# Attention on one Trainium2 core: the two middle batches written out straight in place of a loop

## The chip, the cores and the metric

The kernel runs on one core of one Trainium2 chip. The metric is the device time of one execution in microseconds (us), as the median of a few runs. Lower is better.

## The reference

The reference is one decoder layer over x, of 4 batches with 1024 tokens of 256 channels. Cut to what matters:

```python
x = x + attention(layernorm(x))            # 16 heads of 16, rotary, softmax over 1024 keys
x = x + cross_attention(ctx, layernorm(x)) # 77 context tokens, one head of 256
x = x + experts(layernorm(x))              # 8 experts, 512 tokens each, gelu MLP 256-1024-256
```

The change touches the attention alone, which for each batch b and head h computes

```python
s = q[b, h] @ k[b, h].T * 16 ** -0.5       # 1024 x 1024
out[b, h] = softmax(s) @ v[b, h]
```

## The kernel before, in words

The program has four stages on the chip: `project_qkv`, `attend`, `cross_attend` and `experts`. `attend` holds the softmax attention, and it is the stage that the change touches.

`attend` works through the 4 batches. In each it goes through 4 groups of 4 heads, and for each group through two halves of 512 queries. One group and one half is called a stretch here (`hg` in the code): a batch has 8 of them, and the stage has 32. In a stretch there are 8 key tiles of 128 keys (`kt`). For each key tile TensorE computes the scores of two pairs of heads (L931), ScalarE takes exp of each pair in one instruction of 128x1024 (L750, 16 in a stretch), and TensorE multiplies the result with v (L902). VectorE takes no part in this. It prepares the row maxima that are subtracted in the scores of later stretches: TensorE computes scores of the other orientation into a ring of three PSUM banks (L880, 32 in a stretch) and VectorE reduces each to a maximum (L812). These maxima run 48 items ahead of the scores. Once in a stretch VectorE combines them (L818), TensorE transposes them (L886), VectorE splits them into two parts (L825, L827), and SyncE copies them by 8 small DMAs into two rows of the q stack of the next stretch (L679). The scores of the next stretch wait for these rows (semaphore `s_row`).

GpSimd has two tasks in `attend`. In every even stretch (in the last batch only in the first) it issues 9 DMAs that load a head group's q, k and v for later (L483 and L486), and after them it multiplies the output of the stretch before last with the reciprocal sums (L551, `tail.scale`). The reciprocal sums themselves travel by DMA: L529 for the sums, L535 on VectorE for the reciprocal, L540 and L543 on SyncE to spread them, L558 on SyncE to store the result. ScalarE copies the output bank once in a stretch (L737).

The whole order is written out by hand. Each of the five engines has a function `body(i, first, last)` that emits its program of one batch, with the batch number either a Python number or a loop register. The helper `bodies` calls it. With a Python number every semaphore wait is against a constant and every DMA address is fixed. With a register these are worked out by register instructions beside the work.

At the begin of a body TensorE has the ring in the state that the body before left. `free` decides what it waits for before it writes a bank. From the fourth item on it waits for the reduction of the item three back. For the first three items of a body (`m < NR`) it waits for this:

```python
elif "items" in n:
    pe.wait_ge(s_mr, n["max"])
    pe.wait_ge(s_ra, n["rows"])
```

Here `n["max"]` is the number of all maxima of the bodies before, so the wait is for the last reduction and not for the one three back. This text is the same for a body in the loop and for one outside.

Of the kernel before, what the change touches and what calls it, by code (L numbers as in the profile page):

```python
# [14 lines left out]
B, L, C = 4, 1024, 256  # L15
# [564 lines left out]
def attend(nc, ps, ident, group0, s_clear0, stores, ends, tail, firsts, cw, s_cw, x, ost, wts, qst, kst, vst):  # L580
# [5 lines left out]
    with ctx:  # L586
# [38 lines left out]
        LATE = AHEAD // PER - KT  # L625

        def bodies(eng, body):
            body(0, True, False)
            with eng.Fori(1, B - 1) as i:
                body(i, False, False)  # L630
            body(B - 1, False, True)

        def plan(last):

# [50 lines left out]
        def _(sp):  # L685
# [16 lines left out]
            def body(i, first, last):  # L702
                n = before(i, first)
                for hg in range(NH):
# [14 lines left out]
                    if first and hg == 2:  # L719
                        load_context_weights(sp, cw, s_cw, wts)  # L720
            bodies(sp, body)
            for h in range(2):
                sp.wait_ge(tail.s_os[h], 16 * G * NG)
# [6 lines left out]
        @block.scalar  # L730
        def _(act):
            def take(m, x):

                act.wait_ge(s_pv, KT * (m + 1))
                if not (isinstance(m, int) and m < 2):
                    act.wait_ge(s_att, m - 1)
                nc.scalar.activation(osb[:, x, :], ps[:, PV, :], ACT.Copy).then_inc(s_oe, 1)  # L737

            def body(i, first, last):
                for hg in range(NH):  # L740
                    for kt in range(KT):
                        S = KT * hg + kt
                        for u in range(2):
                            if u == 1 and kt == 1 and not (first and hg == 0):
                                take(8 * i + hg - 1, (hg - 1) % 2)
                            act.wait_ge(s_st[u], 64 * i + S + 1)

                            if not first or S >= NP:
                                act.wait_ge(s_pv, 64 * i + S - NP + 1)
                            nc.scalar.activation(pr[:, S % NP, u], ps[:, 2 * u:2 * u + 2, :], ACT.Exp,  # L750
                                                 scale=D ** -0.5).then_inc(s_ex[u], 1)
            end_leading(act)
            act.wait_ge(s_ra, 1)
            rows(act, 0, 0, (1,))
            bodies(act, body)
            take(NH * B - 1, 1)

        @block.gpsimd
        def _(pool):
# [21 lines left out]
            def body(i, first, last):  # L781
                for hg in range(NH):
# [16 lines left out]
                    if hg > 1 or not first:  # L799
                        tail.scale(pool, g_, 8 * i + hg - 2, hg % 2, 4 * i + (hg - 2) // 2 + 1)  # L800
            bodies(pool, body)
            tail.scale(pool, g_, NH * B - 2, 0, NG * B)

# [1301 lines left out]
```

## Time and profile before

| | us |
|---|---|
| median of 3 runs | 1193.57 |
| the three runs | 1193.57, 1189.91, 1193.67 |
| span of the profiled execution, first to last instruction | 1188.0 |
| median less span | 5.6 |
| first exp of `attend` to the first exp of its last batch | 135.2 to 637.0 |
| TensorE busy, share of the span | 91% |
| VectorE busy, share of the span | 86% |

The span leaves out what lies before the first and after the last instruction of the program. A total for the profiled execution is not given beside its span, so the median stands for it. `attend` takes from about 120 us to about 796 us of the span. The engines' programs are joined by semaphores only, so the stage's pace is seen from the start times of one kind of instruction, here the first exp of a stretch.

### The profile page before, as it was taken

How to read it: one execution, taken by the hardware profiler on the slowest of the kernel's cores; microseconds unless marked ns; L12 is line 12 of the kernel's file. 1: busy time of each engine (PE TensorE's matmuls, PEld its weight loads, DVE VectorE, ACT ScalarE, POOL GpSimd, SP SyncE). 2: the span in 40 equal slices, each digit the busy share in tenths (PEclk: the TensorE clock that was granted, in tenths of full speed). 3: DMA queues.
4: the chain of work that ended last, by engine and by line, in shares of the span. 5: the costliest groups of instructions: out<-in, count | busy, mean ns of one | idle time of the engine just before them, and what ended most of it. 6: DMA issues, size and time to landing. Idle time of an engine off the chain costs nothing. (4 is left out here: it accounts for less than half of the span.)

```text
span 1188.0 us, 24515 instructions
## 1 busy us (share of the span) xinstructions
PE 1086.0 (91%) x8540; PEld 596.5 (50%) x8540; DVE 1021.9 (86%) x2168; ACT 767.9 (65%) x932; POOL 352.7 (30%) x316
## 2 busy tenths in 40 slices
PE   7889989999999998999999999999994059999998
PEld 6776333333333333333333333337784038888897
DVE  8999889999999998999999999827998975766663
ACT  4552368888888886788887888874555014655653
POOL 2657812202220220222022000022100022876575
PEclk9987699999999999999999999999998559999999
DMA  6786664504422440442344000036432022555433
GB/s 238 250 266 219 150 106 97 95 19 78 75 58 38 84 75 19 78 74 45 51 80 78 17 16 16 17 102 211 157 128 95 0 71 57 150 144 132 111 111 36
DMA packets 84695, 114.10 MB, mean 96 GB/s; under 512 B 25056, under 2 KB 57568, under 8 KB 84576
## 3 DMA queue, kind: packets, MB, share of 16 engines
q1 hardware_dynamic: 66256, 69.82, 19.8%
q0 software_dynamic: 15024, 36.17, 17.2%
q10 hardware_dynamic: 3296, 6.56, 1.6%
q8 instruction: 70, 1.15, 0.4%
q14 instruction: 49, 0.40, 0.1%
HBM read 73.31 MB, written 38.27 MB: 94 GB/s over the span
## 5 line engine op out<-in xcount | busy, mean ns | idle before, releaser
L812 DVE TENSOR_REDUCE b_max_halves<-banks 128x1 f32<-128x512 f32 x1024 | 627.1, 680 | 19.9 <-PE banks L880 19.7
L750 ACT ACTIVATE b_probs<-banks 128x1024 f32<-128x1024 f32 x512 | 520.4, 1026 | 153.9 <-PE banks L931 153.8
L880 PE MATMUL banks<-b_k,b_q 62*128 62x512 f32 x1024 | 399.8, 471 | 5.8 <-DVE b_max_halves L812 1.7
L931 PE MATMUL banks<-b_q,b_k 64*128 64x512 f32 x1024 | 386.9, 457 | 8.4 <-DMA b_q<-b_max_rows 5.2
L902 PE MATMUL banks<-b_probs,b_v 128*17 128x256 f32 (+1 forms) x3840 | 316.3, 402 | 0.2 <-ACT b_probs L750 0.2
L931 PEld LDWEIGHTS banks<-b_q,b_k 64*128 64x128 f32 x1024 | 157.1, 186 | 229.7 <-issue 173.3
L880 PEld LDWEIGHTS banks<-b_k,b_q 62*128 62x128 f32 x1024 | 162.2, 190 | 40.4 <-DVE b_max_halves L812 37.4
L902 PEld LDWEIGHTS banks<-b_probs,b_v 128*17 128x17 f32 x3840 | 64.0, 95 | 166.1 <-issue 99.0
L551 POOL TENSOR_TENSOR b_att<-b_out,b_rec_spread 128x512 f32<-128x512 f32 x32 | 41.0, 1283 | 307.6 <-DMA b_rec_spread<-reciprocals 307.4
L483 POOL DMA_DIRECT2D b_q<-q_stacks x60 | 31.8, 532 | 234.6 <-PE banks L902 220.9
L1851 DVE TENSOR_TENSOR e_hTl<-e_hT,e_hTh 128x512 fp32r<-128x512 f32 x64 | 47.6, 745 | 48.2 <-ACT e_hT L1605 46.6
L1631 POOL DMA_INDIRECT e_x<-rows,d_idx x32 | 45.3, 1415 | 110.1 <-DVE d_wx L1806 56.7
L1602 ACT ACTIVATE e_hTh<-banks,e_b 128x512 fp32r<-128x512 f32 x64 | 44.1, 689 | 52.0 <-PE banks L1963 48.4
L1963 PE MATMUL banks<-e_w2h,e_hTh 128*128 128x256 f32 x256 | 73.1, 286 | 0.0
L1963 PE MATMUL banks<-e_w2l,e_hTh 128*128 128x256 f32 x256 | 72.4, 283 | 0.0
L1963 PE MATMUL banks<-e_w2h,e_hTl 128*128 128x256 f32 x256 | 72.4, 283 | 0.0
L1588 ACT ACTIVATE e_xTh<-banks 128x512 fp32r<-128x512 f32 x16 | 8.7, 596 | 83.0 <-PE banks L1951 83.0
L1654 POOL DMA_INDIRECT out_x<-c_x,d_idx x32 | 55.3, 1728 | 17.7 <-DVE c_x L1884 11.0
L1963 PE MATMUL banks<-e_xTh,e_w1h 128*128 128x512 f32 x128 | 53.6, 419 | 3.2 <-DVE e_xTl L1819 2.6
L1963 PE MATMUL banks<-e_xTl,e_w1h 128*128 128x512 f32 x128 | 51.0, 398 | 0.0
L1963 PE MATMUL banks<-e_xTh,e_w1l 128*128 128x512 f32 x128 | 50.6, 395 | 0.0
L392 POOL TENSOR_TENSOR a_rotated<-a_by_even,a_by_odd 128x1024 f32<-128x1024 f32 x13 | 36.4, 2799 | 45.9 <-DVE a_by_odd L331 45.4
(259 smaller groups left out, 1480.5 us busy)
## 6 DMA issues: line engine op xcount, KB each, us to landing
e_w<-in_w SPq DMA_DIRECT2D x16, 1024.0 KB
q_stacks<-a_parts SPq DMA_DIRECT2D x32, 256.0 KB, 4.3
k_stacks<-a_parts SPq DMA_DIRECT2D x32, 256.0 KB, 4.1
b_q<-q_stacks POOLq DMA_DIRECT2D x30, 256.0 KB, 5.7
b_k<-k_stacks POOLq DMA_DIRECT2D x30, 256.0 KB, 6.4
v_tiles<-a_v ACTq DMA_DIRECT2D x8, 544.0 KB, 3.5
b_rec_spread<-reciprocals SPq DMA_DIRECT2D x128, 32.0 KB, 1.8
attended<-b_att SPq DMA_DIRECT2D x128, 32.0 KB, 1.8
```

The source lines that it names most:

```text
L392: g.tensor_tensor(to, by_even[:, q], by_odd[:, q], ALU.add).then_inc(s_eo, 1)
L551: g.tensor_tensor(self.att[:, x, :], self.osb[:, x, :], self.rb[:, x, :], ALU.mult).then_inc(self.s_att, 1)
L750: nc.scalar.activation(pr[:, S % NP, u], ps[:, 2 * u:2 * u + 2, :], ACT.Exp, scale=D ** -0.5).then_inc(s_ex[u], 1)
L812: v.tensor_reduce(mxp[:, (k // NB) % 2, s, p, t, kh:kh + 1], ps[:, bank(last), :], AX.X, ALU.max)\
L880: nc.tensor.matmul(ps[:, bank(last), :], qs[g][stack, p, at:at + P], ks[g][stack, p, CH * kh:CH * kh + CH], start=True, stop=True).then_in ...
L902: last = nc.tensor.matmul(ps[VW * j:VW * j + VS, PV, at], vs[hg // 2][:, kt, j, :], pr[:, S % NP, j // 2, j % 2, at], start=(kt == 0), sto ...
L931: return nc.tensor.matmul(ps[:, 2 * u + s, :], ks[g][stack, u, P * kt:P * kt + P], qs[g][stack, u, CH * h:CH * h + CH], start=True, stop=True)
L1602: nc.scalar.activation(hh[:, f, :], ps[:, UP[f % len(UP)], :], ACT.Gelu, bias=b1[:, x, f:f + 1])
L1631: g.indirect_dma_start(xe[:, x, h, :], None, xrow, bass.IndirectOffsetOnAxis(ap=idx[:, n, h:h + 1], axis=0))\
L1654: g.indirect_dma_start(out, bass.IndirectOffsetOnAxis(ap=idx[:, n, h:h + 1], axis=0), y[:, h, :], None, compute_op=ALU.add).then_inc(s_sc, 16)
L1851: v.tensor_tensor(hl[:, f, :], hf[:, f % NH, :], hh[:, f, :], ALU.subtract).then_inc(s_hl, 1)
L1963: ins = mm(o, a, b, start=(start and m == 0), stop=(stop and m == len(pairs) - 1))
```

## The change

`bodies` in `attend` is the only thing changed. Before, `body` is emitted three times for each engine: for batch 0, for batches 1 and 2 as a hardware loop with the batch number in a register, and for batch 3. After, it is emitted four times, each with a Python number. The arithmetic, its order on each engine, the buffers and the waits stay as they are. The loop of the same name in `experts` is another one and stays.

```diff
         def bodies(eng, body):
-            body(0, True, False)
-            with eng.Fori(1, B - 1) as i:
-                body(i, False, False)
-            body(B - 1, False, True)
+            for i in range(B):
+                body(i, i == 0, i == B - 1)
```

## Rows read from the trace of the kernel before

**Rows 1.** The head of the page: the span and each engine's busy time.

```profile
span 1188.0 us, 24515 instructions
PE 1086.0 (91%) x8540; PEld 596.5 (50%) x8540; DVE 1021.9 (86%) x2168; ACT 767.9 (65%) x932; POOL 352.7 (30%) x316
```

**Rows 2.** Timeline of ScalarE: the first exp of stretches (start, us, ..., idle before).

```profile
283.27 1.02 ACT L750 ACTIVATE b_probs<-banks 128x1024 f32<-128x1024 f32 x1 [0.19 <-PE banks L931]
304.37 1.02 ACT L750 ACTIVATE b_probs<-banks 128x1024 f32<-128x1024 f32 x1 [1.01 <-PE banks L931]
324.58 1.02 ACT L750 ACTIVATE b_probs<-banks 128x1024 f32<-128x1024 f32 x1 [0.19 <-PE banks L931]
...
446.44 1.03 ACT L750 ACTIVATE b_probs<-banks 128x1024 f32<-128x1024 f32 x1 [0.21 <-PE banks L931]
470.25 1.02 ACT L750 ACTIVATE b_probs<-banks 128x1024 f32<-128x1024 f32 x1 [3.70 <-PE banks L931]
494.14 1.02 ACT L750 ACTIVATE b_probs<-banks 128x1024 f32<-128x1024 f32 x1 [1.48 <-PE banks L931]
...
616.04 1.02 ACT L750 ACTIVATE b_probs<-banks 128x1024 f32<-128x1024 f32 x1 [0.21 <-PE banks L931]
636.96 1.02 ACT L750 ACTIVATE b_probs<-banks 128x1024 f32<-128x1024 f32 x1 [0.83 <-PE banks L931]
657.28 1.02 ACT L750 ACTIVATE b_probs<-banks 128x1024 f32<-128x1024 f32 x1 [0.20 <-PE banks L931]
```

**Rows 3.** Instructions of the loop's line: duration ns min/median/max, first and last start.

```profile
L629 PEldq COMPARE_BRANCH  x2: 79/1932/3786, 465.0 to 634.6; - x2
L629 ACTq COMPARE_BRANCH  x2: 40/54/67, 465.6 to 635.2; - x2
L629 ACTq FUSED_REGOPS  x2: 50/53/56, 302.4 to 469.1; - x2
L629 SPq COMPARE_BRANCH  x2: 40/47/54, 471.8 to 639.6; - x2
L629 POOLq COMPARE_BRANCH  x2: 44/51/58, 451.3 to 620.9; - x2
```

**Rows 4.** Timeline at the end of batch 1: TensorE.

```profile
469.08 0.49 PE L931 MATMUL banks<-b_q,b_k 64*128 64x512 f32 x1 [3.06 <-issue]
```

**Rows 5.** Busy time in a window: PE, PEld, DVE, ACT, POOL, PEclk, DMA share, GB/s.

```profile
470.00:475.00 5.00, 5.00 (x37) 1.54 (x36) 3.68 (x7) 2.98 (x4) 0.00 (x0) 0.68 0.10 31
```

**Rows 6.** Timeline 459 to 495 us, around batch 2's first stretch, all engines.

```profile
459.42 1.02 ACT L750 ACTIVATE b_probs<-banks 128x1024 f32<-128x1024 f32 x1 [0.70 <-PE banks L931]
...
481.44 0.93 POOL L486 DMA_DIRECT2D b_v<-v_tiles  x1 [1.93 <-issue]
482.40 1.28 POOL L551 TENSOR_TENSOR b_att<-b_out,b_rec_spread 128x512 f32<-128x512 f32 x1
482.51 1.21 DVE L818 TENSOR_TENSOR b_max<-b_max_halves 128x16 f32<-128x16 f32 x1
483.89 3.04 SPq L558 DMA_DIRECT2D attended<-b_att  x4
485.55 1.02 ACT L750 ACTIVATE b_probs<-banks 128x1024 f32<-128x1024 f32 x1 [1.74 <-PE banks L931]
487.05 5.05 SPq L679 DMA_DIRECT2D b_q<-b_max_rows  x8
493.26 0.49 PE L931 MATMUL banks<-b_q,b_k 64*128 64x512 f32 x1 [1.12 <-DMA b_q<-b_max_rows]
```

**Rows 7.** One line's instructions: duration ns min/median/max.

```profile
L818 DVE TENSOR_TENSOR b_max<-b_max_halves x32: 162/165/1209, 122.8 to 768.6; 128x16 f32<-128x16 f32 x32
```

**Rows 8.** Timeline: GpSimd in the first stretches of batches 1 and 3, TensorE's loads there.

```profile
313.38 1.29 POOL L551 TENSOR_TENSOR b_att<-b_out,b_rec_spread 128x512 f32<-128x512 f32 x1
...
636.19 0.25 PEld L880 LDWEIGHTS banks<-b_k,b_q 62*128 62x128 f32 x2 [0.49 <-DVE b_max_halves L812]
...
645.29 1.29 POOL L551 TENSOR_TENSOR b_att<-b_out,b_rec_spread 128x512 f32<-128x512 f32 x1
```

## Prediction, made before the change was run

> **What bounds the kernel now.** I read the page's head first, then the start times of ScalarE's exp by stretch, then the rows of the loop's own line, and last the timeline around the one place that those point to. The head shows TensorE busy for 91% of the span and VectorE for 86% [rows 1]. Such shares don't say what a loop costs, since the loop's cost is idle time at one or two places. So the pace of `attend` is the view that counts. From the first exp of the second stretch of batch 1 to that of the last one, at 324.58 and 446.44 us, there are six stretches, and each takes (446.44 - 324.58) / 6 = 20.31 us [rows 2]. The first stretch of batch 3, which already is straight code, takes 657.28 - 636.96 = 20.32 us [rows 2]. So inside a body, register waits and constant waits run at one pace, and register arithmetic costs nothing there: the matmuls hide it. What the loop can cost must lie at its edges.
>
> **The edges, with their excess over 20.31 us.**
> - The two stretches around the back edge (batch 1 to 2) take 494.14 - 446.44 = 47.70 us, which is 47.70 - 40.62 = 7.08 us too much [rows 2].
> - The two around the entry (batch 0 to 1) take 324.58 - 283.27 = 41.31 us, 0.69 us too much [rows 2].
> - The two around the exit (batch 2 to 3) take 657.28 - 616.04 = 41.24 us, 0.62 us too much [rows 2].
>
> **Part 1, the back edge's stall.** The loop runs twice, so each engine takes one backward branch. TensorE's compare-and-branch lasts 3786 ns when it is taken and 79 ns when it falls through at the exit [rows 3]. ScalarE's branch starts at 465.6 us and its next register instruction at 469.1, 3.5 us later [rows 3]. TensorE's next matmul starts at 469.08 after 3.06 us of idle time that no other engine ends [rows 4], and the exp of the new batch has waited 3.70 us in place of the usual 0.19 to 0.21, which is 3.5 us more [rows 2]. The branches of TensorE and ScalarE fall together, so the price is one of them and not their sum. SyncE's and GpSimd's taken branches, at 471.8 and 451.3 us, lie away from TensorE's [rows 3], and they are hidden by their waits. Straight code takes no branch. Removed: 3.5 us.
>
> The row for TensorE decides between two rules. The Trainium skill ("Advanced Engine Details and Errata", Control Flow Timing) gives about 108 ns for a compare-and-branch, by which the change would save some 0.1 us at the edge. It also says ("Runtime: NRT & Kernel Launch", Instruction fetch mechanics) that a taken branch to a page of instructions that isn't at hand waits for a fetch of that page. The 79 ns of the exit agree with the first, the 3786 ns of the back edge with the second.
>
> **Part 2, what the stall brings with it.** The second of the two stretches takes 23.89 us, 3.58 too much. It has three pieces.
> - TensorE's granted clock is 0.68 as a mean over 470 to 475 us, with its lower level of 1.2 GHz in a part of it, after the 3 us in which it did nothing [rows 5]. The other two pieces leave 3.58 - 1.04 - 1.28 = 1.26 us for this.
> - GpSimd's load of v comes 1.93 us late, so its multiplication runs at 482.40 to 483.68 [rows 6]. VectorE's combine of the maxima (L818) starts at 482.51 and takes 1.21 us, where the median of 32 is 0.165 [rows 6, 7]. The two overlap there and nowhere else does L818 take so long. The exp at 485.55 waits 1.74 us; the exp at the same place of the stretch before, at 459.42, waits 0.70, so 1.04 us more [rows 6].
> - SyncE stores the output before it copies the new maxima, so both are late: L679 starts at 487.05, 16.8 us into the stretch [rows 6]. The next stretch's first matmul waits 1.12 us for these rows and its exp 1.48 us [rows 2, 6], 1.28 more than usual.
>
> All three follow from one event. Without it batch 2's first stretch should look like that of batches 1 and 3. There the multiplication starts at 313.38 and 645.29 us, 9.0 and 8.3 us into the stretch [rows 2, 8], and ends before the combine, which comes some 11 us into it. Removed: 3.58 us.
>
> **Part 3, what stays.** The excess of 0.62 us at the exit lies at a boundary that takes no branch back. Its cause stands in the code: for the first three items of a body TensorE waits for the last maximum of the body before (`n["max"]`), not for the one three back, so the ring of three banks runs empty once. The trace agrees: at 636.19 us the load of L880 has waited 0.49 us for VectorE [rows 8]. The changed kernel has this wait at all three boundaries. So the boundary from batch 1 to 2 keeps 0.62 us that the stall hid until now, and this must be taken off the gain. The entry goes from 0.69 to 0.62, another 0.07 saved.
>
> **Part 4, what is added.** The instructions of one more body, for each engine. They are as many as are executed today, less the register instructions. Straight batches run at the loop's pace, 20.32 against 20.31 us, so I take nothing for reading them. The bounds of this come from the nearest rows: nothing, or one stall of 3.5 us as at the back edge, if reading ahead falls behind once. I take nothing, since no boundary of batch 3 shows such a wait. On GpSimd the fixed addresses bring the multiplication of an even stretch from 9.0 to 8.3 us into it [rows 2, 8], further from the combine. No transfer is added or moved to another queue, and a gain on GpSimd or SyncE alone is off the path, as they wait there for most of a stretch.
>
> **The sum.** 3.50 + 3.58 - 0.62 + 0.07 = 6.5 us. The stages after `attend` start on its results and so begin that much earlier, with nothing from outside that they wait for. The profiled span becomes 1188.0 - 6.5 = 1181.5 us. The median of the runs is 5.6 us above the span, and I keep that distance: 1193.6 - 6.5 = 1187.1 us. The three runs span 3.8 us, and one lies at 1189.91. About 0.3%, 3.6 us, is what this measurement can tell from no change.
>
> **The rivals.**
> - *The late load returns.* The trace doesn't say why GpSimd's load of v came 1.93 us late. If that is a matter of its own program or queue and not of the back edge, the straight program can have it once too. Against it: of the first stretches of batches 1, 2 and 3 only that behind the back edge shows it. Then 1.04 + 1.28 = 2.3 us stay: 1189.4 us. Chance 0.12.
> - *The boundary's wait is the loop's as well.* If the 0.62 us were due to the loop's header, all excess would go: 7.08 + 0.69 + 0.62 = 8.4 us, 1185.2 us. Against it stands the exit, where the wait names VectorE [rows 8]. Chance 0.06.
> - *The change doesn't do what it says.* If the 3.5 us are a fetch that the straight program needs at the same place, the stall and its train stay, and the time is 1193.5 us. Against it stand the exit's 79 ns and a first stretch of batch 3 without any such wait. The 108 ns of the Trainium skill's "Advanced Engine Details and Errata" (Control Flow Timing) would give this time too. With the chance that the scatter of the runs covers a true gain, 0.15.
> - *Slower: the collision becomes regular.* The two middle batches have 8 even stretches with loads. If GpSimd's multiplication falls on VectorE's combine in each, that costs 2.3 us each, 18.6 in all: 1193.6 - 6.5 + 18.6 = 1205.7 us. It decides from the point where the multiplication starts more than some 9.7 us into a stretch, 1.4 us later than in batch 3's straight code. A delay of that size was seen once. Chance 0.03.
> - The forecast has the remaining 0.64.
>
> **The range.** The cases with a gain reach from 1185.2 to 1189.4 us. The scatter of the runs before, 3.7 us downwards from the median, can lie on either side of that. I give 1183.3 (the forecast less 3.8) to 1190.5, which leaves out most of the case without effect and the slower one. Faster by over 0.3%: 0.81, within 0.3%: 0.15, slower: 0.04.
>
> **What would show it.** Right: no compare-and-branch of this line, no idle time of TensorE over 1 us between batch 1 and 2, a granted clock of 1.00 there, L818 never over 0.3 us, and about 41.2 us for the two stretches around each of the three boundaries, with a wait of about 0.5 us for VectorE at each. Wrong: a new idle time of about 3 us that ends with nothing, anywhere in the four batches; an L818 of over 1 us; a pace of the middle stretches other than 20.3 us; or a longer stretch from the end of `attend` to the end of the kernel than before.

## The result, and the profile after

The changed kernel took 1182.44 us (median of 4 runs, 1181.48 to 1182.80) against 1191.74 us for the kernel before (median of 4, 1189.08 to 1193.67). The ratio is 0.9924, with a 95% interval of 0.9903 to 0.9945. So it is faster, as forecast, but by 9.3 us where 6.5 us were forecast, and the time lies 0.9 us below the range. The idle time, the collision and the wait that the forecast named came out nearly as it said. Most of the miss lies outside them, in the number that the sum was subtracted from.

The head of the changed kernel's page, and its two queues for instructions:

```profile
span 1179.7 us, 22856 instructions
PE 1083.5 (92%) x8540; PEld 595.9 (51%) x8540; DVE 1016.5 (86%) x2168; ACT 768.6 (65%) x932; POOL 352.6 (30%) x316
...
q8 instruction: 65, 1.06, 0.4%
q14 instruction: 40, 0.33, 0.1%
```

The same two queues in the kernel before:

```profile
q8 instruction: 70, 1.15, 0.4%
q14 instruction: 49, 0.40, 0.1%
```

The counts of compute instructions are those of [rows 1]. Only register and branch instructions have gone: 24515 became 22856. The chip also fetched fewer packets of instructions for the straight code, 105 and not 119.

The first exp of the same nine stretches as in [rows 2], from the timeline of ScalarE (start, us, and in brackets the idle time before):

```profile
281.22 1.02 ACT L748 ACTIVATE b_probs<-banks 128x1024 f32<-128x1024 f32 x1 [0.20 <-PE banks L929]
302.16 1.03 ACT L748 ACTIVATE b_probs<-banks 128x1024 f32<-128x1024 f32 x1 [0.83 <-PE banks L929]
322.45 1.03 ACT L748 ACTIVATE b_probs<-banks 128x1024 f32<-128x1024 f32 x1 [0.20 <-PE banks L929]
...
444.26 1.02 ACT L748 ACTIVATE b_probs<-banks 128x1024 f32<-128x1024 f32 x1 [0.18 <-PE banks L929]
465.20 1.03 ACT L748 ACTIVATE b_probs<-banks 128x1024 f32<-128x1024 f32 x1 [0.83 <-PE banks L929]
485.50 1.03 ACT L748 ACTIVATE b_probs<-banks 128x1024 f32<-128x1024 f32 x1 [0.18 <-PE banks L929]
...
607.32 1.03 ACT L748 ACTIVATE b_probs<-banks 128x1024 f32<-128x1024 f32 x1 [0.20 <-PE banks L929]
628.26 1.02 ACT L748 ACTIVATE b_probs<-banks 128x1024 f32<-128x1024 f32 x1 [0.83 <-PE banks L929]
648.58 1.03 ACT L748 ACTIVATE b_probs<-banks 128x1024 f32<-128x1024 f32 x1 [0.19 <-PE banks L929]
```

All three boundaries now look alike. Their two stretches take 322.45 - 281.22 = 41.23, 485.50 - 444.26 = 41.24 and 648.58 - 607.32 = 41.26 us, and the first exp of each batch waits 0.83 us. The boundary between batch 1 and 2 took 47.70 us [rows 2], so it gave 6.46 us; the entry gave another 0.08. Together that is 6.5 us, the forecast sum. The pace between the boundaries is unchanged, (444.26 - 322.45) / 6 = 20.30 us.

A weight load of TensorE at the boundary between batch 1 and 2 (timeline), VectorE's combine in the whole kernel (instructions of one line), and the granted clock at that boundary (a window, with PEclk as the third value from the right):

```profile
464.44 0.26 PEld L878 LDWEIGHTS banks<-b_k,b_q 62*128 62x128 f32 x2 [0.47 <-DVE b_max_halves L810]
```

```profile
L816 DVE TENSOR_TENSOR b_max<-b_max_halves x32: 163/165/175, 121.2 to 759.9; 128x16 f32<-128x16 f32 x32
```

```profile
465.00:470.00 5.00, 4.88 (x46) 1.81 (x48) 5.00 (x9) 4.39 (x6) 1.52 (x3) 1.00 0.23 41
```

The 3.06 us of idle time [rows 4] and the low clock [rows 5] are gone, and the combine's longest is 0.175 us where it was 1.209 [rows 7]. In their place stands the wait of 0.47 us for VectorE that the stall had hidden; it is 0.47 and 0.48 us at the other two boundaries.

GpSimd in the same stretch (timeline):

```profile
473.80 0.93 POOL L486 DMA_DIRECT2D b_v<-v_tiles  x1 [1.20 <-issue]
474.75 1.29 POOL L551 TENSOR_TENSOR b_att<-b_out,b_rec_spread 128x512 f32<-128x512 f32 x1
```

The load of v is late here too, by 1.20 us. It is not of the back edge's making. The multiplication that follows ends at 476.04 us, 10.84 us into the stretch, and the combine starts at 10.99: the collision of [rows 6] was missed by 0.15 us.

### The profile page after: what moved, and what is told of

It reads as the page before. It is cut to its first block and busy times, and to the rows that moved or that the text cites. A ratio compares the mean times of both kernels' runs of the same rounds, so it can differ in the third digit from the quotient of the medians.

```text
span 1179.7 us, 22856 instructions
## 1 busy us (share of the span) xinstructions
PE 1083.5 (92%) x8540; PEld 595.9 (51%) x8540; DVE 1016.5 (86%) x2168; ACT 768.6 (65%) x932; POOL 352.6 (30%) x316
## 5 line engine op out<-in xcount | busy, mean ns | idle before, releaser
L1849 DVE TENSOR_TENSOR e_hTl<-e_hT,e_hTh 128x512 fp32r<-128x512 f32 x64 | 47.6, 745 | 48.3 <-ACT e_hT L1603 48.3
```

The source lines that it names most:

```text
L1849: v.tensor_tensor(hl[:, f, :], hf[:, f % NH, :], hh[:, f, :], ALU.subtract).then_inc(s_hl, 1)
```

## The experiments

### Where the kernel before scatters

The first experiment is the kernel before, with no edit.

> The kernel before, unchanged, to see where its scatter lies (1189.1 to 1193.7 us in four runs, while the changed kernel's four lay within 1.3 us). Theory 'the profiled execution was one of the fast ones, and the extra 3.7 us of the others belongs to the back edge': runs in two groups near 1190 and 1193.6 us, time less span near 1.8 us in each, and in a trace the two stretches around the back edge take 47.7 us or more (up to 51). Theory 'the scatter lies in the first stage, before attend': the trace shows the first exp at 133 to 139 us and the two stretches at 47.7 in each.

Measured: 1190.75 us (12 runs, 1186.4 to 1194.4). Another 28 runs of the same kernel on this chip have a median of 1189.24. In all the runs of the experiments, of every kernel, the time is 1.64 to 1.87 us above the span. There are no two groups, but a spread of 8 us. The three longest of these 40 runs (over 1194 us) have a granted clock of 0.942 to 0.945 as a mean over the run, the three shortest (under 1187 us) one of 0.950. None of those over 1194 us has a trace, so the stage in which they lost clock isn't seen. The first exp of the three stretches around the back edge in this trace:

```profile
444.23 1.02 ACT L750 ACTIVATE b_probs<-banks 128x1024 f32<-128x1024 f32 x1 [0.19 <-PE banks L931]
467.65 1.03 ACT L750 ACTIVATE b_probs<-banks 128x1024 f32<-128x1024 f32 x1 [3.32 <-PE banks L931]
490.51 1.02 ACT L750 ACTIVATE b_probs<-banks 128x1024 f32<-128x1024 f32 x1 [1.76 <-PE banks L931]
```

Two stretches take 46.28 us here, 1.4 less than in the first trace, and less than both theories gave. The window after the stall shows the main difference:

```profile
470.00:475.00 5.00, 5.00 (x40) 1.65 (x40) 4.79 (x9) 4.37 (x5) 3.57 (x7) 1.00 0.45 112
```

The granted clock stays at 1.00, where the first trace had 0.68 [rows 5]. So the stall's price varies from one execution to the next. The late load, the combine of 1.21 us and the late maxima are all in this trace too. Its second stretch takes 490.51 - 467.65 = 22.86 us, so at full clock these together cost 22.86 - 20.31 = 2.55 us, where the prediction counted 1.04 + 1.28 = 2.32. If they cost the same in the first trace, that leaves 1.0 us of its 3.58 for the low clock, and not 1.26.

### The loop on some engines only

Three kernels keep the loop for a part of the engines and give the others straight code:

```diff
-        def bodies(eng, body):
+        def bodies(eng, body, loop=False):
+            if loop:
+                body(0, True, False)
+                with eng.Fori(1, B - 1) as i:
+                    body(i, False, False)
+                body(B - 1, False, True)
+                return
             for i in range(B):
                 body(i, i == 0, i == B - 1)
...
-            bodies(pe, body)
+            bodies(pe, body, loop=True)
```

> Loop for TensorE's program alone, straight code for the other four. Theory 'the stalls of the engines fall together and TensorE's alone is enough': the two stretches around the back edge take 41.2 + 2.9 (stall less the boundary's own wait) + about 1.3 for the slow clock = 45.4 us if VectorE's combine isn't hit, 47.7 if it is; TensorE's compare-and-branch again 3.8 us; total 4 to 6.5 us above the changed kernel, 1186.5 to 1189 us. Rival 'the stall is ScalarE's or VectorE's': 41.2 us and 1182.4 us.

> Loop for ScalarE, VectorE, GpSimd and SyncE, straight code for TensorE. Theory 'ScalarE and VectorE pay a fetch of the same length, in parallel': TensorE soon runs out of reduced banks and of exps, so the two stretches take 45 to 47.7 us, nearly as in the loop on all engines, 1186 to 1190 us. Rival 'only TensorE's branch stalls the stage': 41.2 us and 1182.4 us.

> Loop for GpSimd and SyncE alone. Theory 'their branches are hidden': 1182.4 us, the two stretches at 41.2 us. The late load of v in batch 2's first stretch (1.9 us before, 1.2 us in the changed kernel too): if it were due to GpSimd's loop, it would be larger here than 1.2; I expect 1.2 again, since the straight kernel has it as well, and no collision with VectorE's combine, or one that costs 2.3 us if the register instructions' 0.7 us are enough to push the multiplication into it (9.55 + 0.7 = 10.25 us into the stretch, until 11.5, over the combine at 10.98).

| loop on | time, us (runs) | ratio to before, 95% interval | two stretches around batch 1 to 2 |
|---|---|---|---|
| all five (before) | 1189.24 (28) | | 46.3 to 48.6 in four traces |
| TensorE | 1187.31 (10) | 0.9983, 0.9974 to 0.9992 | 46.22 |
| all but TensorE | 1187.55 (9) | 0.9977, 0.9963 to 0.9992 | 45.50 |
| GpSimd and SyncE | 1184.23 (4) | 0.9958, 0.9943 to 0.9972 | 42.31 |

TensorE's branch in the kernel that loops on TensorE alone, then ScalarE's and VectorE's branches and the register instructions behind them in the one that loops on all but TensorE, with that kernel's combine (timeline), and last GpSimd and VectorE in the one that loops on GpSimd and SyncE (timeline):

```profile
L630 PEldq COMPARE_BRANCH  x2: 79/1815/3551, 464.2 to 632.1; - x2
```

```profile
L630 DVEq FUSED_REGOPS  x2: 63/63/63, 302.5 to 468.7; - x2
L630 ACTq FUSED_REGOPS  x2: 50/53/56, 302.5 to 467.9; - x2
L630 ACTq COMPARE_BRANCH  x2: 40/54/67, 465.4 to 632.6; - x2
L630 DVEq COMPARE_BRANCH  x2: 55/64/72, 465.5 to 632.7; - x2
```

```profile
481.34 1.21 DVE L822 TENSOR_TENSOR b_max<-b_max_halves 128x16 f32<-128x16 f32 x1
```

```profile
477.21 0.93 POOL L486 DMA_DIRECT2D b_v<-v_tiles  x1 [1.93 <-issue]
478.17 1.28 POOL L551 TENSOR_TENSOR b_att<-b_out,b_rec_spread 128x512 f32<-128x512 f32 x1
478.29 1.21 DVE L822 TENSOR_TENSOR b_max<-b_max_halves 128x16 f32<-128x16 f32 x1
```

TensorE's stall alone is enough for nearly the whole price: 46.22 - 41.24 = 4.98 us, where the loop on all engines gives 5.0 to 7.4. ScalarE and VectorE stall without it too, for 2.5 and 3.2 us between branch and next register instruction. That kernel's 45.50 us are 4.26 too many, but they hold a collision as well (the combine of 1.21 us), and GpSimd's and SyncE's loops give a collision by themselves. Against the kernel that loops on these two alone, ScalarE's and VectorE's loops add 45.50 - 42.31 = 3.19 us. The stalls run side by side, and straight code on one side alone gains 1.7 to 1.9 us of the 7. The value of 46.22 us lies between the two that I had given. The low clock lasted longer than assumed, with a granted clock of 0.72 in 465 to 470 us and 0.60 in 470 to 475, and the combine was not hit.

GpSimd's and SyncE's branches are hidden, but their register instructions are not quite: they and a load that is late by 1.93 us and not 1.20 put GpSimd's multiplication onto the combine. That cost 42.31 - 41.24 = 1.07 us. I had expected 41.2 us without a collision and 2.3 us more with one. The late maxima, the other 1.3 us of [rows 2, 6], did not come, in this kernel or in the one that loops on all but TensorE. So they don't follow from the collision alone. Before SyncE copies the maxima it stores the output (L558, 4 DMAs), and these four took it 1.88 us in both kernels, against 2.9 to 3.4 us in the four traces of the kernel before. In `before_again` the multiplication ends as early in the stretch as here (12.1 and 12.2 us into it), and the copy still starts 15.8 us into it and not 14.4. Why the four stores take longer there, no run shows. The kernel's time is 1.8 us above the changed kernel's first median, of which the collision accounts for 1.07.

### Is it the branch, or the way back?

This kernel is the changed one with a loop of two turns and nearly no body, put between batch 1 and 2 in every engine's program:

```diff
             for i in range(B):
+                if i == 2:
+                    with eng.Fori(0, 2):
+                        eng.wait_ge(s_minus, 1)
                 body(i, i == 0, i == B - 1)
```

> The straight kernel with a loop of two turns that holds one satisfied wait, put between batch 1 and 2 in all five programs. Theory 'the branch itself is cheap, the 3.8 us are the fetch of a body that is no longer at hand': a taken compare-and-branch of 0.3 us or less on TensorE, as the loop in the experts has (244 ns), the two stretches around the boundary at 41.2 to 42 us, and the time of the changed kernel plus 0 to 1 us. Rival 'a taken branch empties the engine and costs 3 to 4 us whatever its target': 44 to 47 us for the two stretches, 1186 to 1189 us.

Measured: 1184.52 us (7 runs, 1180.22 to 1187.53), ratio 0.9953, 0.9936 to 0.9970. The rows of the small loop's line on TensorE, and of the loop in `experts` in the kernel before:

```profile
L630 PEldq COMPARE_BRANCH  x2: 76/220/365, 463.7 to 464.3; - x2
```

```profile
L1545 PEldq COMPARE_BRANCH  x2: 76/160/244, 1082.9 to 1135.1; - x2
```

The same taken branch at the same place lasts 365 ns with a short body, against 3516 to 3837 ns with the long one. The two stretches take 486.30 - 445.05 = 41.25 us, and the first exp waits 0.83 us as without the loop. So it is not the branch as such that costs. What the stall may wait for is seen in the traffic of the kernel before between 464.9 and 469.1 us (the DMA queues, with packets, MB and share):

```profile
q8 instruction: 1, 0.02, 2.1%
q1 hardware_dynamic: 152, 0.01, 2.0%
q14 instruction: 2, 0.02, 1.2%
```

Three packets of instructions were moved in it, and three engines (TensorE, ScalarE and VectorE) had just branched. The kernels with a part of the loop say which queue is whose. With the loop on TensorE alone the whole kernel moves 70 packets on q8 and 40 on q14, and with the loop on all but TensorE 65 and 49; the straight kernel has 65 and 40. The traffic of these two kernels in their stalls, first TensorE's (464.2 to 467.8 us), then ScalarE's and VectorE's (465.4 to 467 us):

```profile
q1 hardware_dynamic: 147, 0.01, 2.1%
q8 instruction: 1, 0.02, 1.9%
```

```profile
q14 instruction: 2, 0.02, 3.1%
```

So q8 goes with TensorE's loop and q14 with ScalarE's and VectorE's, and in each stall a packet came for each engine that had branched. This agrees with the fetch that the Trainium skill describes ("Runtime: NRT & Kernel Launch", Instruction fetch mechanics): a taken branch to a page of instructions that is not at hand waits until a DMA has brought it. It is an agreement of queue, count and time. Packets of instructions also come where nothing stalls (one on q8 between 460 and 466 us in the changed kernel), and no run changes the fetch and leaves the loop as it is, so the fetch as the cause is argued and not shown.

The kernel's median is 2 to 4 us above the two medians of the changed kernel, where I had expected 0 to 1. No row of the boundary explains it; its one trace is of the second shortest of its 7 runs (1182.87 us), so this stays open. The kernel of the extra load below, measured on the same chip, has a boundary of 41.24 us and a median of 1184.31 too, so such a difference also comes without this loop.

### The wait at the start of a body

```diff
                 elif "items" in n:
-                    pe.wait_ge(s_mr, n["max"])
-                    pe.wait_ge(s_ra, n["rows"])
+                    ago = NR - 1 - m
+                    tail_ = (START if n["items"] == len(START) else plan(False)[1])
+                    tail_ = tail_[len(tail_) - ago:]
+                    pe.wait_ge(s_mr, n["max"] - count(tail_, "max"))
+                    pe.wait_ge(s_ra, n["rows"] - count(tail_, "rows"))
```

It is put on top of the changed kernel. The first three items of a body now wait for the reduction of the item three back, as all others do: the edit takes off the wait's target the items that come after that one.

> The changed kernel with the boundary's wait made exact: the first three items of a body wait for the item three back and not for the last one. Theory 'the 0.62 us at each boundary is this wait': the first exp of a batch comes without extra wait, each pair of stretches around a boundary takes 40.6 us, three times 0.62 = 1.9 us less than the changed kernel, 1180.5 us. Rival 'it is something else at a boundary, as the reciprocal that VectorE computes there, which every stretch has': no change.

> The changed kernel, unchanged, for its scatter. The kernel before spreads over 1186.4 to 1194.4 us in 40 runs; time less span was 1.64 to 1.87 us in all of them. Theory 'most of that scatter comes from the back edge' (how long the low clock after the stall lasts, whether the late load hits the combine): the changed kernel stays within 2 us, 1181 to 1183. Rival 'it comes from the stages before the second stretch, which the change leaves alone': a spread of some 3 to 5 us here too, 1180 to 1186, with a median near 1183. In the trace: three boundaries at 41.2 us for their two stretches, and the 11th load of v late by 1.2 us again.

Measured on one chip: 1179.89 us with the exact wait (5 runs, 1179.56 to 1181.43; ratio to before 0.9917, 0.9903 to 0.9932), 1180.78 us for the changed kernel (5 runs, 1180.18 to 1182.46; ratio 0.9927, 0.9912 to 0.9943). The first exps of the exact wait's kernel around batch 1 to 2:

```profile
444.43 1.02 ACT L748 ACTIVATE b_probs<-banks 128x1024 f32<-128x1024 f32 x1 [0.21 <-PE banks L932]
464.75 1.03 ACT L748 ACTIVATE b_probs<-banks 128x1024 f32<-128x1024 f32 x1 [0.22 <-PE banks L932]
485.04 1.02 ACT L748 ACTIVATE b_probs<-banks 128x1024 f32<-128x1024 f32 x1 [0.20 <-PE banks L932]
```

The two stretches take 40.61 us, and 40.62 and 40.61 at the other two boundaries. The excess is gone altogether, on average 0.63 us at each of the three. The cause of the 0.62 us is shown. In the median it gave 0.9 us and not 1.9; the two kernels' runs overlap, so the size of the gain is from the trace alone. This kernel has the lowest median of the study. The changed kernel's five runs here lie within 2.3 us, a little more than the first theory gave; with the two runs further below it is 4.2 us over 11 runs, against 8 us over the 61 of the kernel before.

### What makes the load of v late

```diff
             load(0, 2)
+            pool.dma_start(vs[3][:].rearrange("p t h d -> p t (h d)"),
+                           vst[0][:, :, 0:G * VS]).then_inc(s_ld[3], 16)
```

The waits on `s_ld[3]` are raised by 16, and GpSimd waits for this load before it fills the buffer properly.

> The changed kernel with one load of v more on GpSimd's queue, issued before batch 0 into a buffer that is overwritten later. In all traces so far the 11th load of v is late, by 1.2 us in straight programs and 1.9 us in looped ones. Theory 'GpSimd's queue wraps after a fixed amount of descriptors': the late one moves one load earlier, to the one in the last even stretch of batch 1 (the 10th of the regular loads, near 431 us). Rival 'it is a place in GpSimd's program': the one near 474 us stays late. The time says nothing here, within 1182 to 1186 us.

GpSimd in the last even stretch of batch 1 and in the first of batch 2 (timeline):

```profile
435.06 0.93 POOL L486 DMA_DIRECT2D b_v<-v_tiles  x1 [1.02 <-issue]
...
475.28 0.92 POOL L486 DMA_DIRECT2D b_v<-v_tiles  x1
```

The late one has moved one load earlier, and the one that was late in all other traces comes at once. So it goes with how much GpSimd's queue has been given (or how many loads of v), not with a place in the program and not with the back edge. What the queue does there, no run shows. The time was 1184.31 us (4 runs, 1183.3 to 1185.1), within what I had given.

### More traces of both kernels

The traces left 1 to 2 us between the medians without a place. So each kernel was traced twice more, on one chip.

> The kernel before, a third trace of it, for the 1 to 2 us between the kernels' medians that the boundaries don't explain. Theory 'the back edge costs a varying amount': the two stretches around it take between 46.3 us (no low clock after the stall, as in the second trace) and 49 us, and the start of batch 0's third stretch lies at 179 to 182 us as in the changed kernel's traces. Rival 'the loop's kernel is slower before its loop too': that start is over 181 us.

> As before_3: 46.3 to 49 us for the two stretches around the back edge; 179 to 182 us for the start of the third stretch.

> The changed kernel, a third trace of it. Both theories: 41.2 us for the two stretches around each boundary. Theory 'the back edge costs a varying amount': the third stretch of batch 0 starts at 178.8 to 182 us. Rival 'the loop's kernel is slower before its loop too': always under 180 us.

> As after_3: 41.2 us for the two stretches around each boundary; the start of the third stretch at 178.8 to 182 us, or always under 180 us by the rival.

From the first exps of the stretches and the end of the last exp in eight traces, in us:

| trace | time | third stretch of batch 0 starts | two stretches around batch 1 to 2 | from the last exp to the end |
|---|---|---|---|---|
| before, 1st to 4th | 1189.9, 1186.4, 1187.7, 1190.5 | 181.4, 179.8, 179.3, 181.3 | 47.7, 46.3, 47.6, 48.6 | 394.5, 394.8, 394.6, 395.0 |
| after, 1st to 4th | 1181.5, 1180.4, 1184.0, 1184.4 | 179.5, 178.8, 181.5, 182.0 | 41.2, 41.3, 41.2, 41.2 | 394.8, 394.9, 395.4, 395.5 |

The first time of the kernel before is that of the one run that fits the trace's span, 1189.91. The windows after the stall in the fourth trace of before:

```profile
465.00:470.00 5.00, 1.90 (x16) 0.79 (x12) 1.56 (x4) 0.98 (x1) 0.00 (x0) 0.77 0.11 27
470.00:475.00 5.00, 5.00 (x34) 1.49 (x36) 3.30 (x6) 2.64 (x3) 0.00 (x0) 0.55 0.05 14
```

The granted clock fell earlier and stayed low longer there than in the first trace, and this is the longest of the four boundaries. Between them, the four traces give a back edge of 46.3 to 48.6 us, a mean of 47.6, and the changed kernel 41.2 in each. The rival is out: the changed kernel reaches its third stretch as late as 182.0 us, so the loop doesn't slow what lies before it. What varies there, 178.8 to 182.0 us, varies in both kernels.

The eight traces also say where their own difference lies. The spans of the four traces of before are 1186.8 us on average and those of the changed kernel 1180.8, a difference of 6.05 us. The boundary gives 6.3 of it. The start of the third stretch differs by under 0.1 us on average and the rest of `attend` by 0.1. The part after the last exp is 0.4 us longer in the changed kernel on average (394.7 and 395.2 us). The prediction had named a longer end as a sign of being wrong; the two kernels' values overlap, so nothing is shown by this.

## Why the prediction was wrong in its time, and right in most of its steps

- **Part 1, the stall, was right.** It is gone, the branch itself is cheap (365 ns with a short body), and TensorE's stall alone brings nearly the whole price.
- **Part 2, what the stall brings, was right for this execution and taken for a constant.** 3.58 us were there in one trace. In four traces the whole excess of the two stretches over the changed kernel is 5.0, 6.4, 6.5 and 7.4 us. That the first pair of traces gives 6.5 us exactly is so because the forecast was read from that very execution; the mean of the four is 6.3. Within the 3.58 us the low clock was put too high (1.26 us, 1.0 by `before_again`) and the other two pieces too low (2.32, 2.55 there). The sentence "All three follow from one event" was wrong in two pieces. The late maxima need more than the collision: SyncE's four stores took 2.9 to 3.4 us where they came and 1.88 us where they didn't. And the load of v is late without the back edge too. In the loop it is later by another 0.7 us, and the register instructions ahead of it add 0.7 us more; that is enough for a collision even without a stall.
- **Part 3, the wait that stays, was right**: 41.24 us for a forecast of 41.24, and an edit of the wait alone removes it, where the prediction had only the code and one row for it.
- **Part 4 was right.** Straight code kept the pace of 20.3 us, no new idle time came at the boundaries, and fewer packets of instructions were fetched.
- **The sum, 6.5 us, was right, and the step to the time was wrong.** "The median of the runs is 5.6 us above the span, and I keep that distance" is the term that failed. The profiled execution was not the median one. In all runs that have a span beside the time it is 1.64 to 1.87 us above it. By that the profiled execution took about 1189.8 us, which fits the run of 1189.91 and not the two of 1193.6. So 3.8 of the 4.7 us between forecast and result are in this term. From there the same steps give 1188.0 + 1.8 - 6.5 = 1183.3 us, which is 0.9 us above the first median and within the runs of the changed kernel (11 runs, 1180.2 to 1184.4, median 1182.3). The median 1193.57 of three runs stood high: over the 61 runs of the kernel before in this study the median is 1189.4, and 5 of them are over 1193. 1189.4 - 6.5 = 1182.9. The range was built around the same term: it took the scatter of 3.8 us off the forecast itself and not off the lowest case with a gain (1185.2), so it ended above the result.
- **Rival 1** (the late load returns) was right that the late load is not the back edge's, and wrong in what it costs: the load was late, the collision was missed by 0.15 us, and 2.3 us were not paid. A collision without the stall costs 1.07 us. That nothing was paid hung on those 0.15 us. **Rival 2** (the boundary's wait is the loop's) is refuted by the 0.83 us wait before the first exp in straight code, and **rival 3** by the missing stall. **Rival 4** (a regular collision) did not come; in straight code the multiplication starts at 8.2 to 8.4 us in all even stretches that load but the one with the late load.
- **What stays open.** The pooled medians differ by 1189.4 - 1182.3 = 7.1 us, and the two direct comparisons give 1191.74 - 1182.44 = 9.3 and 1189.65 - 1180.78 = 8.9 us. The boundaries give 6.3 us as a mean of four traces. In the eight traces nothing else is left over (6.05 us between the spans), so the rest, 1 to 3 us, is a matter of executions without a trace. The traced ones of the kernel before were rather short (a mean of 1188.6 us against the median of 1189.4), and either kernel varies by 3 us before its third stretch. No row assigns the rest.

## What to carry to other kernels

Subtract a gain that was read from a trace from the time of the execution that was traced, and look at how far single runs of the kernel lie apart before you trust a median of three. A loop in hardware costs nothing in its body here, but one taken branch back over a long body cost a stall on each busy engine and what followed from it. The stalls ran side by side, so the loop must go from all busy engines at once to give most of the gain: straight code on one side gave 1.7 to 1.9 us of 7. A wait that a stall has hidden comes back when the stall goes: look for it at a boundary that has no stall and take it off the gain.

## What the runs showed of the hardware

- A taken branch on TensorE: 3516 to 3837 ns over the long body of `attend`, 244 ns over the shorter one in `experts`, 365 ns over a body of one wait, 76 to 79 ns when not taken.
- After TensorE's idle time of 2.80, 3.06, 3.08 and 3.10 us at the same place, its granted clock in the windows 465 to 470 and 470 to 475 us was 1.00 and 1.00, 0.98 and 0.68, 0.75 and 0.91, 0.77 and 0.55 in four executions of one kernel. In the loop on TensorE alone it was 0.72 and 0.60 after 2.81 us.
- VectorE's combine, of 0.165 us by itself, took 1.21 us where it started 0.11 or 0.12 us after GpSimd's multiplication of 128x512 (482.40 and 478.17 us), and both times it ended 0.05 us or less after that multiplication's end. In `tiny_loop` it started 0.15 us before the multiplication's end, took 0.20 us and ended 0.05 us after it. So where they overlap it ends with GpSimd's instruction; what holds it up, no run shows.
- GpSimd's 11th regular load of v came 1.2 us late in straight code (1.5 in `tiny_loop`) and 1.9 us late where GpSimd's program was a loop, in every trace but that of `extra_load`, where one load of v more ahead of it moved the lateness to the 10th.
- 4 DMAs of SyncE (L558) took 1.7 to 2.0 us in most stretches and 2.5 to 3.4 in others, with the same shapes. No run shows what decides it.
